# Ordering the edges of a three-layer graph network by scattered records instead of matrix products

## The reference

```
h = relu(layernorm(x))                       # x: 10000 x 512
for l in 0, 1, 2:
    p   = relu(h @ Wp.T + bp)                # wanted only for the source rows of edges
    agg = segment_sum(p[src], dst); cnt = segment_sum(1, dst)
    y   = (agg / max(cnt, 1)) @ Wl.T + bl + h @ Wr.T
    h   = layernorm(relu(y)) * g + be        # not after layer 2
out = x + y
```

## Time and profile before

| | us |
|---|---|
| runs, median of 3 | 1559.97 (1559.12 to 1561.4) |
| profiled execution | 1554.35 |
| its span | 1552.6 |
| PE busy | 1522.5 (98%) |
| DVE, ACT, POOL busy | 969.3, 718.7, 562.4 |
| node stage of layer 0, first product to the turn of step 68 | about 17 to 258 |

### The profile page before, as it was taken

The page is one execution under the profiler, slowest core; times in us unless marked ns, Lnnn a source line. Parts: engine busy times, 40 slices in busy tenths (PEclk is TensorE's granted clock), DMA queues, the critical chain, the costliest instruction groups (busy, mean ns, idle before and its releaser), DMA issues.

```text
span 1552.6 us, 21851 instructions
## 1 busy us (share of the span) xinstructions
PE 1522.5 (98%) x7518; PEld 1244.2 (80%) x7518; DVE 969.3 (62%) x2158; ACT 718.7 (46%) x1367; POOL 562.4 (36%) x528
## 2 busy tenths in 40 slices
PE   6999999999999999999999999999999999999996
PEld 5777887888888788888888888878888888888885
DVE  7877785655555575776565555557666675555552
ACT  5766642232323575767423233347576662232221
POOL 2655434344422100100244442224353366444323
PEclk9999999999999999999999999999999999999999
DMA  9887774554554687888555545479999987445434
GB/s 326 298 305 241 251 242 153 153 89 88 89 93 58 169 280 248 272 280 286 188 155 91 93 87 90 61 190 321 323 328 326 326 299 215 86 86 92 70 47 54
DMA packets 150605, 289.13 MB, mean 186 GB/s; under 512 B 18456, under 2 KB 18496, under 8 KB 150496
## 3 DMA queue, kind: packets, MB, share of 16 engines
q1 hardware_dynamic: 123040, 223.76, 42.4%
q0 software_dynamic: 26880, 62.93, 23.3%
q10 hardware_dynamic: 576, 1.05, 0.2%
HBM read 130.89 MB, written 156.78 MB: 185 GB/s over the span
## 4 chain that ended last, share of the span: by engine, by line
PE 96%; DMA 2%; POOL 1%; issue 0%; SPq 0%; ACT 0%; DVE 0%; POOLq 0%
PE bank L703 14%; PE bank L704 14%; PE bank L702 14%; PE bank L690 10%; PE bank L816 7%; PE bank L817 7%; PE bank L818 7%; PE bank L839 7%; PE bank L837 7%; PE bank L838 7%; DMA out<-rows_out,into_i 1%; DMA rows_in<-node_x,sorted_src 1%; PE bank L751 1%; PE bank L788 1%; PE bank L797 0%
## 5 line engine op out<-in xcount | busy, mean ns | idle before, releaser
L702 PE MATMUL bank<-w_high,h_low 128*128 128x512 f32 x900 | 374.8, 416 | 0.0
L703 PE MATMUL bank<-w_low,h_high 128*128 128x512 f32 x900 | 358.2, 398 | 0.0
L704 PE MATMUL bank<-w_high,h_high 128*128 128x512 f32 x900 | 356.5, 396 | 0.0
L973 ACT ACTIVATE h_high<-h_pre 128x500 fp32r<-128x500 f32 x120 | 74.7, 622 | 450.0 <-DVE h_pre L1272 450.0
L581 POOL DMA_INDIRECT rows_in<-node_x,sorted_src x120 | 121.0, 1008 | 267.4 <-PE bank L690 201.8
L704 PEld LDWEIGHTS bank<-w_high,h_high 128*128 128x128 f32 x900 | 170.2, 189 | 39.2
L1063 DVE TENSOR_TENSOR h_low<-bank,h_high 128x512 fp32r<-128x512 f32 x152 | 105.0, 691 | 148.5 <-ACT h_high L919 146.2
L702 PEld LDWEIGHTS bank<-w_high,h_low 128*128 128x128 f32 x900 | 171.0, 190 | 31.2 <-DVE w_low L1052 0.2
L703 PEld LDWEIGHTS bank<-w_low,h_high 128*128 128x128 f32 x900 | 171.4, 190 | 30.6
L816 PE MATMUL bank<-xt_low,w_high 128*128 128x500 f32 x480 | 194.7, 406 | 0.0
L837 PE MATMUL bank<-w_high,h_low 128*125 128x512 f32 x480 | 190.1, 396 | 0.6 <-DVE h_low L1278 0.6
(11 more groups left out here) (131 smaller groups left out, 2351.7 us busy)
## 6 DMA issues: line engine op xcount, KB each, us to landing
node_x<-xn SPq DMA_DIRECT2D x237, 256.0 KB, 3.4
rows_in<-node_z SPq DMA_DIRECT2D x158, 256.0 KB, 4.1
node_z<-rows_out SPq DMA_DIRECT2D x142, 256.0 KB, 2.1
out<-rows_out SPq DMA_DIRECT2D x79, 256.0 KB, 3.1
rows_in<-x SPq DMA_DIRECT2D x78, 256.0 KB, 3.8
residual<-x SPq DMA_DIRECT2D x78, 256.0 KB, 3.9
node_z<-bias_z SPq DMA_DIRECT2D x16, 256.0 KB, 3.5
rows_in<-node_x SPq DMA_DIRECT2D x16, 256.0 KB, 2.6
```

Source lines behind the costliest of these rows:

```text
L702: nc.tensor.matmul(psum, low[:, k, :], w_high("r", l)[:, k, :], start=(k == 0), stop=False)
L703: nc.tensor.matmul(psum, high[:, k, :], w_low("r", l)[:, k, :], start=False, stop=False)
L704: last = nc.tensor.matmul(psum, high[:, k, :], w_high("r", l)[:, k, :], start=False, stop=(k == K - 1))
```

## The change

- **Groups of four.** Ranks are taken among 500 keys, the segmented sum may run through four tiles, the accumulating DMAs wait for all earlier ones at every fourth tile. There are 512 spare rows in place of 256; clearing them takes four DMAs in place of two.
- **No sort products.** `order_mask`, `number_b_of`, `sort`, `sorted_row`, `carry_of` and the two small products of `next_and_steps` go. DVE turns the ranks into row numbers (`rows_of`, 5 small instructions every eighth step). POOL scatters a 16-byte record (src, dst+1, cnt) of each edge to that row of a DRAM table (`store_edges`, 40 indirect DMAs of 125 records) and reads the table back in order (3 DMAs), once plainly and once shifted by one edge.
- **Lookup first.** The counts are looked up for the edges as they come, in steps 27 to 46. Two tiles are counted per step, in steps 3 to 22.
- **Carry.** In step 62 DVE makes src, targets, 1/cnt and the comparison with the next edge; in step 63 PE turns the 125x40 comparison, in step 64 DVE copies it; POOL stores it (40x125 bf16) and loads it back to all 128 partitions (1.28 MB). After that come the gathers.
- **Startup.** In layer 0 tiles 0 to 9 pass through statistics, mean, normalising, storing two steps later and tiles 10 to 19 one step later, seen from their product. In all layers DVE makes the statistics after the small terms, not before. The keys for the ranks are made in step -1 (was -5) and loaded in steps 1 to 5 in five parts (was -1 to 2 in four).

```diff
-STEP_ROWS_FLOAT = -5
-STEP_LOAD_ROWS = -1
+LATER = (10, 20)
+STEP_ROWS_FLOAT = -1
+STEP_LOAD_ROWS = 1
+COUNTS = 2
-STEP_RANK = 4
-STEP_SORT = 6
-STEP_SORTED = 47
-STEP_LOOKUP = 50
+STEP_RANK = 5
+STEP_COUNTED = 24
+STEP_LOOKUP = 27
+STEP_SORTED = 62
...
+        def units_at(l, p):
+            units = []
+            for n in range(max(0, p - len(LATER)), min(p + 1, product_count[l])):
+                if n + (sum(n < c for c in LATER) if l == 0 else 0) == p:
+                    u = unit_of[l][n]
+                    units += [u] + ([u + 1] if u + 1 < NODE_TILES and tile_of[l][u + 1] >= product_count[l] else [])
+            return units
...
-                if e and t % PAIR == 0:
+                if e and t % GROUP == 0:
                     all_added(pool, e)
...
+            def store_edges(t):
+                pool.wait_ge(rows_placed, t // SPREAD + 1)
+                pool.wait_ge(count_read, t + 1)
+                if t == 0:
+                    pool.wait_ge(edges_done, 2)
+                G.indirect_dma_start(
+                    out=edge_table, out_offset=bass.IndirectOffsetOnAxis(ap=row_i[0:EDGE_ROWS, t:t + 1], axis=0),
+                    in_=edges[0:EDGE_ROWS, t, :], in_offset=None).then_inc(edges_stored, DMA)
+
+            for t in range(EDGE_TILES):
+                count_masks(t)
+            stored = 0
             for t in range(EDGE_TILES):
                 reach_mask(t)
+                if t == EDGE_TILES // 2:
+                    for k in range(K):
+                        split_l(0, k)
+                if t % LOOKUPS == LOOKUPS - 1 and t >= 2 * LOOKUPS:
+                    store_edges(stored)
+                    stored += 1
+            for t in range(stored, EDGE_TILES):
+                store_edges(t)
+            pool.wait_ge(edges_stored, DMA * EDGE_TILES)
+            pool.wait_ge(pads_done, 7)
+            table = edge_table.rearrange("(p t) c -> p t c", t=EDGE_TILES)
+            G.dma_start(in_order[0:EDGE_ROWS, :, :], table).then_inc(order_loaded, DMA)
+            G.dma_start(in_next[0:EDGE_ROWS - 1, :, :], table[1:EDGE_ROWS, :, :]).then_inc(order_loaded, DMA)
...
+            pool.wait_ge(carry_copied, 1)
+            G.dma_start(carry_table, carry_row[0:EDGE_TILES, :]).then_inc(carry_stored, DMA)
+            pool.wait_ge(carry_stored, DMA)
+            G.dma_start(carry[:].rearrange("p t e -> p (t e)")[:, 1:EDGE_TILES * EDGE_ROWS],
+                        carry_table.rearrange("(a t) e -> a (t e)", a=1)[:, 0:EDGE_TILES * EDGE_ROWS - 1]
+                        .to_broadcast([P, EDGE_TILES * EDGE_ROWS - 1])).then_inc(carry_loaded, DMA)
...
             def rank(t):
...
-                                       in0=dst_row[0:EDGE_ROWS, k * PAIR:(k + 1) * PAIR, :],
+                                       in0=key_row[0:EDGE_ROWS, g * GROUP:(g + 1) * GROUP, :],
...
-                    for u in units_at(l, i + AHEAD_STATS):
-                        node_stats(l, u)
                     for u in units_at(l, i + AHEAD_STD):
                         node_rstd(l, u)
                     for u in units_at(l, i + AHEAD_MEAN):
                         node_mean(l, u)
                     for u in units_at(l, i + AHEAD_STD):
                         node_off(l, u)
+                    for u in units_at(l, i + AHEAD_STATS):
+                        node_stats(l, u)
```

More of the change, by code:

```diff
@@ L353, in all_added @@
         def all_added(eng, tiles):
-            for a in range(PAIR):
-                eng.wait_ge(e_added[a], DMA * tiles // PAIR)
+            for a in range(GROUP):
+                eng.wait_ge(e_added[a], DMA * tiles // GROUP)
         def all_xn_stored(eng, l):
@@ L500, in _ @@
                         for table in (node_z, out):
-                            sp.dma_start(table[PAD_NODE:TABLE_ROWS, :].rearrange("(a p) d -> p a d", p=P), zeros
-                                         ).then_inc(spare_stored, DMA)
+                            for a in range(0, GROUP, 2):
+                                sp.dma_start(table[PAD_NODE + a * P:PAD_NODE + (a + 2) * P, :]
+                                             .rearrange("(a p) d -> p a d", p=P), zeros).then_inc(spare_stored, DMA)
                     if l == 0 and i == 1:
@@ L645, in _ @@
-            for k in range(K):
-                split_l(0, k)
-            pool.wait_ge(row_sorted, PAIRS)
+            def store_edges(t):
[6 more added lines that the diff above has]
+                    in_=edges[0:EDGE_ROWS, t, :], in_offset=None).then_inc(edges_stored, DMA)
@@ new lines, in _ @@
+            pool.wait_ge(edges_stored, DMA * EDGE_TILES)
[3 more added lines that the diff above has]
+            G.dma_start(in_next[0:EDGE_ROWS - 1, :, :], table[1:EDGE_ROWS, :, :]).then_inc(order_loaded, DMA)
+            last, first = (b.rearrange("p (g a) c -> p g (a c)", a=GROUP)
+                           for b in (in_next[EDGE_ROWS - 1:EDGE_ROWS, :, :], table[0:1, :, :]))
@@ new lines, in _ @@
+            G.dma_start(last[:, :, 0:4 * (GROUP - 1)], first[:, :, 4:4 * GROUP]).then_inc(order_loaded, DMA)
+            pool.wait_ge(carry_copied, 1)
[4 more added lines that the diff above has]
+                        .to_broadcast([P, EDGE_TILES * EDGE_ROWS - 1])).then_inc(carry_loaded, DMA)
@@ L849, in _ @@
                         node_product(l, i)
-                    if l == 0 and 0 <= i - STEP_COUNT < EDGE_TILES:
-                        count(i - STEP_COUNT)
-                    if l == 0 and 0 <= i - STEP_SORT < EDGE_TILES and (i - STEP_SORT) % PAIR == PAIR - 1:
-                        sort((i - STEP_SORT) // PAIR)
+                    if l == 0 and 0 <= i - STEP_COUNT < EDGE_TILES // COUNTS:
+                        for q in range(COUNTS):
+                            count((i - STEP_COUNT) * COUNTS + q)
+                    if l == 0 and i == STEP_COUNTED + 1:
+                        steps_of_counts()
                     if l == 0 and i == STEP_SORTED + 1:
-                        next_and_steps()
+                        turn_carry()
                     if l == 0 and STEP_LOOKUP <= i < STEP_LOOKUP + EDGE_TILES // LOOKUPS:
@@ new lines, in graph_digits @@
+                V.tensor_scalar(edges[:, :, 1], dst_f[:], 1.0, None, ALU.add).then_inc(edges_done, 1)
+                for a in range(GROUP):
+                    last = V.tensor_scalar(of_group(key_f[:], a), of_group(dst_f[:], a), float(KEY), edge_no[:, a:a + 1],
+                                           ALU.mult, ALU.add)
+                last.then_inc(digits, 1)
+            def rank(t):
+                g = t // GROUP
+                if t == 0:
+                    dve.wait_ge(digits, 5)
+                else:
+                    dve.wait_ge(placed, t)
@@ new lines, in edges_in_order @@
+            def edges_in_order():
+                number = in_order[:, :, 1]
+                dve.wait_ge(order_loaded, 3 * DMA)
+                V.tensor_copy(sorted_src[:], in_order[:, :, 0]).then_inc(src_ready, 1)
+                V.tensor_tensor(continues[0:EDGE_ROWS, :], in_next[0:EDGE_ROWS, :, 1], number[0:EDGE_ROWS, :], ALU.is_equal
+                                ).then_inc(continues_done, 1)
+                V.reciprocal(share[0:EDGE_ROWS, :], in_order[0:EDGE_ROWS, :, 2]).then_inc(share_done, 1)
+                for a in range(GROUP):
+                    last = V.tensor_scalar(of_group(to_spare[:], a), of_group(number, a), -1.0,
@@ L1379 @@
     dst_cols = given("dst_cols", columns(inputs["dst"], rows))
-    dst_rows = given("dst_rows", np.asarray(inputs["dst"]).reshape(tiles // PAIR, PAIR * rows))
+    dst_rows = given("dst_rows", np.asarray(inputs["dst"]).reshape(tiles // GROUP, GROUP * rows))
     weights = []
```

345 lines of the change are left out of this document (140 added, 205 removed).

## The result

The changed kernel takes 1549.84 us (median of 6 executions, 1545.74 to 1552.39), the kernel before beside it 1561.19 (6, 1559.12 to 1561.83): ratio 0.9927, 95% interval 0.9912 to 0.9941, 11.35 us or 0.73% less. In a second set it was 0.9937 (0.9920 to 0.9954). Faster, as forecast, but by half of the 22.1 us, and outside the range of 1532 to 1546.

What follows compares the result with a forecast made beforehand. PE was taken as the bound, busy 1522.5 of 1552.6 us. Terms -12.5 - 0.2 - 7.0 - 3.4 - 2.5 + 3.0 + 0.5 = -22.1 us gave 1537.9 us, with an eight-in-ten range of 1532 to 1546.

Steps and rivals of the forecast that it cites:

- the three signs by which the prediction called itself wrong: Wrong if DVE waits for the table, PE waits over 2 us for layer 0 gathers, or rank-and-lookup steps exceed 3.8 us.
- Sort products and gathers: Layer 0: removed sort products -12.5 us and -0.2 in steps 48 and 63; wait for the first gathers gone, -7.0.
- Start: Start of the kernel: first product near 14.2 us instead of 16.96, taken as -2.5 us (0 to -3).
- End: End of the kernel: the last accumulating DMA goes with its rows, no longer waiting for earlier ones, -3.4 us.
- Scatters: POOL's chain: 1.5 us per scatter, 22 after the last mask, 14 us in hand before DVE asks in step 62.
- the slower rival: Scatters late, from 2.15 us each: DVE waits in step 62 and PE behind it, 1564.8 us; chance 0.05.
- At nothing: ... 1 MB more of zeros in step 20: The additional stores of zeros in step 20 were costed at no time.
- I give this 3 us more for DVE in 17 steps: Steps 28 to 44: collisions of DVE with POOL's masks and the four low parts of Wl, 3 us (0 to 8).
- DVE's sum of 60.2 against 58.7 us: Steps 28 to 44: DVE's work of 60.2 us against PE's 58.7, so DVE may fall behind by about 1.5 us.
- I take +0.5 (0 to 7): Carry load of 1.28 MB ahead of layer 0's gathers in the same queue: 4 to 6 us, costing 0.5.
- The rival: Wait for layer 0's gathers comes back behind the carry load, 7.0 us lost again, 1544.4 us; chance 0.16.
- Two rivals of 0.16 each: Gathers' wait returns behind the carry load, 1544.4 us; DVE bounds steps 28 to 47, 8 us of collisions, 1542.9 us.

Runs made afterwards that it cites:

- edits 2, 3 and 6: Changed kernel with the four subtractions moved behind the sorted edges' loads, the carry load in two parts and the zero stores spread over steps 30 to 42: ratio 0.9836.
- experiment 9: Three kernels, each the changed kernel with three edits at a time, two of them with the zeros spread: ratios 0.9854, 0.9836 and 0.9846.
- experiments 6 and 7: Each one edit to the changed kernel: 6 issues the zero stores in steps 30 to 42, ratio 0.9895; 7 restores the first tiles' one-per-step order, 0.9907.
- experiment 8: Changed kernel with the adds into the table waiting for all earlier adds at every second tile, not every fourth: ratio 0.9948.
- Experiment 1: The changed kernel run again without any edit, against the kernel before: ratio 0.9937, 1544.84 us.
- experiments 3 and 4: Each one edit to the changed kernel: 3 cuts the carry load in two parts, ratio 0.9877; 4 issues it whole, two steps earlier, 0.9887.
- edit 2: Changed kernel with POOL's four subtractions moved from among the reach masks to behind the three loads of the sorted edges: ratio 0.9851.
- experiment 11: Kernel with subtractions moved, carry load split, zeros and one-column products spread, given the old order of the first tiles' statistics: ratio 0.9842, against 0.9804 without that.
- experiment 5: Changed kernel with the first lookup, and with it all lookups, one step later (28, not 27): ratio 0.9910.

## Why the prediction was wrong

The forecast was 22.1 us less and the kernel gave 11.35: the gains came, and three costs were sized at 3.5 us that measure about 15. Two of the three signs by which the prediction called itself wrong were there, PE's wait for the gathers of layer 0 (2.96 and 0.33 us) and steps with ranks and lookups over 3.8 (5.40, 7.63, 5.62); DVE never waited for the table.

The gains, step by step. Here the kernel with the three losses removed (edits 2, 3 and 6) is put beside the kernel before.

- *Sort products and gathers.* From the tenth turn of layer 0 to the start of layer 1 the difference grows by 20.6 us: 13.3 to the last turn of the node stage, 7.3 behind it. The forecast was 12.5 + 0.2 and 7.0, 19.7 in all (20 times 0.62 is 12.4). Right, to 0.9 us, with the ranks over 500 keys in it.
- *Start.* -2.5 forecast, -3.1 to -3.3 at the fourth to tenth turn. A little more.
- *End.* -3.4 forecast, 3.65 less 0.27 = 3.4 measured. Right.
- *Scatters.* 1.5 us by estimate, 1.49 measured, far under the 2.15 from which the slower rival decided. A 16-byte write's extra cost, if there is one, is not seen in the pitch. In the one trace that has the landings (experiment 9, with the zeros spread) a scatter landed in 3.9 us and a gather in 3.5 (medians).

The costs, in the changed kernel:

- *"At nothing: ... 1 MB more of zeros in step 20"* failed. It cost 2.5 us by the steps, and I had named nothing that hides it. It needed the later order beside it, which brings a second tile's store and load into one step near there: with the zeros spread or with the old order ACT's wait of 5.2 us went.
- *"I give this 3 us more for DVE in 17 steps"* was the right mechanism in a wrong shape. Masks of 0.6 us cost nothing that can be measured: with the block away no rank takes over 0.92 us. DVE's sum of 60.2 against 58.7 us cost nothing either, since the steps are 3.45 once its lead is whole. What cost was one event, the four subtractions back to back, for which I had the row: 5.06 us. The price of a rank beside them is up to their whole length, and with the lower clock behind it 6.4 us of PE. The Trainium skill, page "SBUF — State Buffer", section "Who interferes with whom", describes an exclusive lock; the trace agrees, 5.52 us against 4.97. But the rank is not always kept out so long. In experiments 6 and 7 it came through behind the first subtraction (1.87 us, and POOL's second took 1.72 in place of 1.28); in experiment 8 it took 0.72, and POOL's last 1.80. Nor does the earlier start decide: the rank began 0.02 us ahead of the block where it took 5.52, and 0.04 ahead where it took 1.87. What does is not shown.
- *"I take +0.5 (0 to 7)"* for the carry load: measured about 6.4, near the upper end. The load itself was put at 4 to 6 us and took 8.9. The rival named the right transfer and price, but the wrong victim. I looked at what is behind the load in its own queue, the gathers. What it delayed was a store on another queue, for which all gathers wait. Experiment 1 shows that store landing in 8.8 us behind the load, and experiments 3 and 4 that it lands sooner as less of the load is ahead of it; it was the last thing before the barrier.

Sum: 2.5 + 5.9 to 6.4 + 6.4, about 15 us, where 3.5 had been allowed. -22.1 + 11.5 less 1.5 for the better gains makes about -12; measured 11.35, 10 and 11.3. Two rivals of 0.16 each came true together, by their prices: 6.5 for the gathers, and 8 in place of 3 for collisions, though DVE was never the bound. I had treated them as alternatives; a range that reaches only to one of them could not hold both. Both prices on top of the forecast give 1537.9 + 6.5 + 5.0 = 1549.4, beside the 1549.84 measured. That closeness is in part luck, since the zeros are in neither.

Open: where the executions of edit 2 without a trace kept the higher clock, what the remote waits are, 2 us of experiment 11, what decides how long the block holds a rank, and what holds the last scatter. Not tried: the four subtractions set apart from one another, with masks between them, in their old place.

## What to carry to other kernels

When a transfer is added, ask what on any queue must land in the same 10 us, and above all for the last store before a barrier. A wait of TensorE of 1.8 to 1.9 us cost 2.0 where the clock stayed up and 3.7 where the lower one followed (experiments 2 and 5); one of 3.8 to 4.1 cost 5.9 to 6.4. Long POOL work with two inputs belongs where DVE has no two-input work; whether it does less harm with gaps in it was not tried. Independent small risks happen together, so add their prices into the range.

## What was not expected of the hardware

- A DVE operation of 0.72 us took 5.52 and 5.87 us beside four POOL operations of 1.25 to 1.29 us each; in other phases the same block stretched it to 1.25 or 1.87 only, or not at all (0.72), and POOL's operation took 1.72 or 1.80.
- A 256 KB store landed in 2.3 us in a quiet stretch, but in 8.8 behind a 1250 KB broadcast load on another queue (POOL went on 9.6 to 9.7 us after its issue), and in 7.5 us (median, the kernel of experiment 5 from 84 to 110 us) where the engines moved 401 GB/s.
- The same kernel takes 0.4% longer on one chip than on two others, and only traces of that level have waits ended by something remote, 0.3 to 8 us each, on ACT and POOL and once on DVE.
- 3.6 us of one-column products had the lower clock with them or behind them in 20 of 26 cases, 2.3 us on the step behind them in the one shown; split into four times 0.95 us, in none of 8.
- The executions of the changed kernel in experiment 1 differ by 5.6 us, and the mean granted clock goes with it: 1545.6 to 1547.0 us at 0.991, 1541.4 to 1544.1 at 0.992 to 0.994.
